# Decoder layer on one core: the order and the filling of TensorE's prologue

## The reference, cut to what matters

```python
def reference(x, ctx_2048, ...):
    x = _layernorm(x + attn(x, qkv_w, qkv_b, ..., proj_w, proj_b, norm_w))   # quantised weights: sign(w) * mean|w|
    x = _layernorm(x + xattn(x, ctx_2048, Wq, Wk, Wv, Wsk, Wsv, Wo))
    x = _layernorm(x + ffn(x, base_w, base_b, router_w, router_b, lora_A, lora_B))
    return x

def _bitlinear(x, w, b):
    w_scale = jnp.maximum(jnp.mean(jnp.abs(w)), 1e-05)
    x_scale = jnp.maximum(jnp.max(jnp.abs(x), axis=-1, keepdims=True), 1e-05)
    x_q = jnp.round(x / x_scale * 127.0)
    return jnp.einsum('...i,oi->...o', x_q, jnp.sign(w)) * (x_scale * w_scale / 127.0) + b
```

## Time and profile before

| what | value |
|---|---|
| median of 3 runs | 913.03 us (912.97 to 913.53) |
| the profiled execution | 913.3 us |
| its span | 911.2 us |
| PE busy | 802.1 us (88%) |
| DVE busy | 509.5 us (56%) |
| ACT busy | 326.4 us (36%) |
| DMA, whole span | 27.10 MB, mean 30 GB/s |

### The profile page before, as it was taken

How to read it: one execution, slowest core, us unless ns; L and a number is a source line. 1 busy time by engine, 2 the same in 40 slices (tenths; PEclk the granted TensorE clock), 3 DMA queues, 4 the chain that set the end, 5 groups by cost and what they waited for, 6 DMA issues and landing times.

```text
span 911.2 us, 22548 instructions
## 1 busy us (share of the span) xinstructions
PE 802.1 (88%) x10161; PEld 524.5 (58%) x10209; DVE 509.5 (56%) x1060; ACT 326.4 (36%) x424; POOL 85.5 (9%) x103
## 2 busy tenths in 40 slices
PE   3788878888998989988998989988998979999996
PEld 2466763477445864577445864577445864486443
DVE  4756584448745593748745593648745582435143
ACT  5534224333245224433245224433245124310422
POOL 1111011000300021000300021000300010010001
PEclk9989999999999999999999999999999999997998
DMA  9921000100002000010002000010001000000000
GB/s 345 246 55 47 2 2 1 47 2 2 2 1 70 3 2 1 26 47 2 1 1 71 3 2 1 27 46 1 1 1 48 2 1 1 24 1 1 1 24 23
DMA packets 19022, 27.10 MB, mean 30 GB/s; under 512 B 5608, under 2 KB 7784, under 8 KB 18928
## 3 DMA queue, kind: packets, MB, share of 16 engines
q1 hardware_dynamic: 18784, 25.64, 9.1%
q10 hardware_dynamic: 144, 0.03, 0.0%
HBM read 21.47 MB, written 4.19 MB: 28 GB/s over the span
## 4 chain that ended last, share of the span: by engine, by line
PE 63%; DVE 19%; ACT 12%; issue 4%; POOL 1%; DMA 1%; ACTq 0%; POOLq 0%; SPq 0%; DVEq 0%
ACT p_b L761 7%; PE ps L1148 7%; PE ps L1184 6%; PE ps L1065 6%; PE ps L1225 6%; DVE max_b L1487 6%; PE ps L1113 4%; PE ps L1048 3%; PE ps L1085 3%; PE ps L893 2%; DVE max_a L1385 2%; PE ps L968 2%; PE ps L1173 2%; PE ps L1157 2%; PE ps L978 2%
## 5 line engine op out<-in xcount | busy, mean ns | idle before, releaser
L761 ACT ACTIVATE p_b<-ps 128x2048 f32<-128x2048 f32 x64 | 106.5, 1664 | 115.9 <-PE ps L1157 115.9
L1487 DVE TENSOR_REDUCE max_b<-ps 128x4 f32<-128x768 f32 (+2 forms) x160 | 106.6, 711 | 31.1 <-PE ps L1127 19.3
L1363 DVE SCALAR_TENSOR_TENSOR nat<-ps,st_a,qkv_bias 128x512 f32<-128x512 f32 x48 | 35.7, 744 | 98.0 <-PE ps L893 96.8
L1113 PE MATMUL ps<-qk_b 32*128 32x192 f32 (+2 forms) x1024 | 65.5, 341 | 22.9 <-DVE max_b L1487 16.8
L1148 PE MATMUL ps<-qk_b 32*128 32x512 f32 (+1 forms) x512 | 66.2, 586 | 9.7 <-ACT p_b L761 5.2
L1113 PEld LDWEIGHTS ps<-qk_b 32*128 32x128 f32 x1024 | 46.2, 188 | 39.9 <-DVE max_b L1487 27.3
L1225 PE MATMUL ps<-base_t,x_t 128*128 128x512 f32 x128 | 63.8, 624 | 0.0
L1173 PE MATMUL ps<-p_b,v_b 128*32 128x256 f32 (+1 forms) x1024 | 61.7, 358 | 2.4 <-ACT p_b L761 2.0
L1048 PE MATMUL ps<-c_t,wq 128*128 128x256 f32 x256 | 60.6, 385 | 2.4 <-DVE out_a L1408 2.3
L1065 PE MATMUL ps<-x_t,wq 128*128 128x256 f32 x256 | 61.3, 385 | 0.0
L1184 PE MATMUL ps<-wo,o_fb 128*128 128x512 f32 x128 | 59.0, 599 | 0.8 <-DVE o_fb L1529 0.8
(11 more groups left out here) (207 smaller groups left out, 1432.7 us busy)
## 6 DMA issues: line engine op xcount, KB each, us to landing
x_in<-x SPq DMA_DIRECT2D x8, 512.0 KB, 5.4
p_b<-ctx SPq DMA_DIRECT2D x8, 512.0 KB, 4.6
y<-x SPq DMA_DIRECT2D x7, 512.0 KB, 3.3
p_b<-L_attn_qkv_w SPq DMA_DIRECT2D x2, 1024.0 KB, 6.5
p_b<-L_xattn_Wq SPq DMA_DIRECT2D x1, 2048.0 KB, 14.9
x<-L_attn_qkv_w SPq DMA_DIRECT2D x2, 512.0 KB, 9.5
x<-L_ffn_base_w SPq DMA_DIRECT2D x2, 512.0 KB, 10.2
wo<-L_xattn_Wo SPq DMA_DIRECT2D x8, 128.0 KB, 9.1
```

Of the source, the lines that this page charges most:

```text
L761: act.activation(p_b[:, j % 2, :, 0:cols], ps[:, 4:8, 0:cols], ACT.Exp, scale=DB ** -0.5).then_inc(pb_here.sem, 1)
L1113: pe.matmul(bank(4 + r)[:, (i % 2) * N:(i % 2) * N + 2 * n * S], q_b[strip[r], i, :, :].rearrange("p h q -> p (h q)"), k_b[strip[r], half, ...
L1363: dve.scalar_tensor_tensor(nat[:, t, w, :], bank(nat_bank(b, w)), st_a[:, 2, t:t + 1], qkv_bias[:, w * C:(w + 1) * C], ALU.mult, ALU.add). ...
L1487: ins = dve.tensor_reduce(max_b[:, half, 0, i:i + k, 2 * n:2 * n + 2], ps[:, 4 + 2 * n:6 + 2 * n, :].rearrange("p r (i n) -> p i r n", i=2 ...
```

## The change

Two things change, all in the prologue and all on PE. `a1(0)` moves ahead of `early` in PE's list. And a helper `warm(n)` is added, n matmuls of the identity with itself repeated four times (512 columns, bfloat16) into bank 7. It runs 22 of them ahead of the wait for the signs of piece 0, 3 ahead of piece 1, 11 ahead of a1(0)'s wait for the rounded x, and 3 in `early` ahead of the wait for the third piece.

```diff
+            def warm(n):
+                for _ in range(n):
+                    pe.matmul(bank(7).rearrange("p (a n) -> p a n", a=4), eyeb, eyeb.unsqueeze(1).to_broadcast([P, 4, P]), start=True, stop=True)
+
             for n in range(2):
+                warm((22, 3)[n])
                 pe.wait_ge(signed.sem, n + 1)
                 sign_turn(n)
...
             def early(b):
+                warm(3)
                 pe.wait_ge(signed.sem, 4)
                 sign_turn(2)
                 pe.wait_ge(cf_in.sem, 16)
...
             def a1(b):
+                if isinstance(b, int) and b == 0:
+                    warm(11)
                 x_round(pe, b)
                 za_here.before(pe, b)
...
-            first = [(-1, early), (0, a1), (0, of(a1_qkv, 0, [0])), (0, of(a1_qkv, 0, [1])), (0, of(a1_qkv, 0, [2])), (0, of(a1_qkv, 1, [0])),
+            first = [(0, a1), (-1, early), (0, of(a1_qkv, 0, [0])), (0, of(a1_qkv, 0, [1])), (0, of(a1_qkv, 0, [2])), (0, of(a1_qkv, 1, [0])),
```

## The result

| runs of one set | kernel before, median | changed kernel, median | ratio, 95% interval |
|---|---|---|---|
| first set, 20 and 20 runs | 915.22 us (911.13 to 915.94) | 911.16 us (907.95 to 914.61) | 0.9970 (0.9958 to 0.9982) |
| second set ("again"), 29 and 12 runs | 913.17 us | 912.75 us | 0.9989 (0.9974 to 1.0005) |
| third set ("again2"), 32 and 12 runs | 913.70 us | 910.75 us | 0.9971 (0.9958 to 0.9983) |

The account below looks back on a forecast made before the run. The prediction took the chain up to 31 us, with PE not its only engine, as the bound. Terms 2.7 + 0.5 + 0.6 = 3.8, less 0.4, gave 3.4 us: 913.0 to 909.6 us, range 907.2 to 912.3 us.

Parts of the forecast that it names:

- What bounds the kernel: Up to 31 us: PE is not alone on the chain; x's transposes wait 3.6 us for work they don't need.
- The fill ahead of piece 0: Prologue: 22 fills from 3.3 to 10.2 us raise the clock, costing 0.5 us on the chain (bounds 0 and 3.0).
- The move of x: Prologue: x transposed under ACT's signs, so the first real matmul begins at 18.6 us instead of 21.30, 2.7 us earlier.
- DVE becomes the bound: After the first nat: DVE sets the pace, the sixth nat ending at 27.5 instead of 31.28 us, 3.8 us earlier.
- What is late next: Behind the sixth nat, to L837: the ctx load and the clock's fall do not move with the chain; 0.4 us lost.
- the cap of 4.9 us: At ctx's landing, 51.4 us: the load costs nothing up to a total gain of 4.9 us, and caps it there.
- the 0.4 us set against it: Score matmuls at 44.8 us (old time): 1.1 us lost if the clock falls before them, otherwise nothing; taken as 0.4.
- The sum: Whole kernel: 2.7 + 0.5 + 0.6 = 3.8, less 0.4, a gain of 3.4 us, from 913.0 to 909.6 us.
- the term for the late part: The rest of the program, eight batches: no transfer is waited for, so it should follow unchanged.
- A worse late part: Rival, low clock at 817 to 831 us: the stretch grows or another appears, some 3 us back, 912.6 us; chance 0.07.
- The slower rival: Prologue: identity products don't raise the clock, fills delay everything, 5.3 us slower, 918.3 us; chance 0.05.
- Nothing arrives: Rival: a later wait that doesn't move takes up the prologue's shift, leaving 913 us; chance 0.05.

Follow-up runs that it names:

- again: The changed kernel run once more, unaltered, against the kernel before: 912.75 us, ratio 0.9989.
- again2: The changed kernel run unaltered another time, on one chip with three rivals, against the kernel before: 910.75 us, ratio 0.9971.
- fill12: The changed kernel with 12 fills instead of 22 ahead of piece 0: 910.42 us, ratio 0.9963 to the kernel before.
- fill12_tail: The changed kernel with 12 first fills, plus five keep_on matmuls ahead of the last batch's first score group: 909.89 us, ratio 0.9954.
- fill_turns: The changed kernel with each fill matmul of 512 columns replaced by 4 transposes of 128 columns: 912.81 us, ratio 0.9990.

## Why the prediction was right or wrong

**What bounds the kernel.** Right. The transposes of x waited for work that they don't need. One reading was wrong, without a consequence for the sum: what lands at 8.83 us is the second weight piece. The first was there at 6.1 us, which this row of ACT in the kernel before shows:

```profile
6.12 1.91 ACT L599 ACTIVATE x_t<-p_b 128x2048 bf16<-128x2048 f32 x1 [3.67 <-DMA p_b<-L_attn_qkv_w]
```

The order alone takes the start from 145.0 to 141.7 us.

**The fill ahead of piece 0.** Begin 3.3 (3.55 us), end 10.2 (10.3 us), piece 0's copy 11.3 (11.23 us): right for this profile. But the identity's load was taken as a fixed 2.6 us; it was 2.8 and 4.0 us in two profiles of the same kernel, and the fills began between 3.33 and 4.92 us in six. The lower level lasted for a varying part of the 22: they took 6.34 to 7.57 us. The cost on the chain was 0.5 us forecast; by fill12 it is 0 to 1.5 us, within the bounds that the prediction gave.

**The move of x.** The 11 fills did not start behind piece 1's transposes but at 13.25 us, behind ACT's first copy, which PE's program waits for there; x was transposed from 15.62 us, still under ACT's signs. Forecast 18.6 us for the first real matmul, 17.92 us measured. ACT's copy of x began at 16.66 us, since it overlaps the end of the signs, and the 0.51 us between the copy and the first matmul, which I carried over from the earlier trace rows, were 0.24 us; what made up the 0.51 us was not looked into. The first nat was at 19.06 us (forecast 19.7).

**DVE becomes the bound.** Nearly right. The sixth nat's end was forecast at 27.5 us, and measured at 26.2. DVE had one wait of 0.26 us, ahead of the sixth nat; from the first nat to the sixth's end it took 7.15 us with that wait, and not 7.75 us, because nat and L1373 overlap by some 0.1 us where I had added gaps. Both engines end together here.

**What is late next.** The ctx load was waited for, 0.62 us, under the cap of 4.9 us, as forecast. The fall of the clock came with the idle stretch, as forecast; the 0.4 us set against it can't be seen apart. From the sixth nat (5.1 us) to the start (4.7 us) 0.4 us were lost in this profile.

**The sum.** Forecast 3.4 us; at the start, the mean of six profiles of the changed kernel (141.1 us) is 3.9 us under the mean of four of before (145.0 us), from 2.4 to 5.4 us by pairs. The mechanism and its size at the start were right, and two errors offset each other in it: the sixth nat came 4.7 us earlier on average (30.6 and 25.9 us) and not 3.8, and 0.7 us of that were lost before the start and not 0.4.

**The step that failed** is the term for the late part and the base under it. The sum put the late part at nothing ("should follow unchanged") and took 913.03 us as the base, both on one ground: "The three runs agree within 0.6 us, so it is steady from run to run". They agreed by chance. Single runs of the kernel before go from 910.9 to 916.1 us with the median of the first set at 915.22 us, and its late part takes 69.8 or 71.3 us. So 913.03 us was no fair base. A worse late part, which I priced at 3 us and gave 0.07, is common: 1 profile in 6 of the changed kernel, 1 in 4 of before and 10 in 10 of the other kernels, at 1.0 to 3.3 us each. That the measured 911.16 us is only 1.6 us from the forecast is in part luck: the gain was taken from a base that was 2.2 us too low.

How much of the gain at the start the late part took back is worked out and not shown. The means are 911.7 us (44 runs) and 914.0 us (116 runs). Less 2.1 us outside the span, 696.3 us, and the starts of 141.1 and 145.0 us, that leaves late parts of 72.2 and 70.6 us. By this working the start gained 3.9 us and the late part gave back 1.6 us, which makes the 2.3 us between the means. It rests on starts read in six and four profiles, and these are no fair sample: the six profiled executions of the changed kernel took 909.9 us on average, 1.8 us under its mean of all runs, and the four of before 913.7 us, 0.3 us under. Later starts in the runs without a profile would do as well. Why a shift at the start would lengthen the late part on average, and whether it does beyond chance, stays open.

**The slower rival** (products of the identity don't raise the clock) is out: the 22 fills took 6.34 to 7.57 us in six profiles of the changed kernel, where at the lower level 9.4 us would have passed. "Nothing arrives" is out as well.

## What to carry to other kernels

Take a step that waits in an engine's queue behind work it does not need, and move it; that was worth 3.3 of 3.9 us at the start here, without one extra instruction. Fill matmuls that keep the clock up must end before the data that the engine waits for, and when they end hangs on the load that they start from and on when the clock rises. And before a base time is trusted to a few tenths of a per cent, look at whether the time has more than one length; find two marks in the trace by which the span splits, and compare kernels mark by mark.

## What the runs showed of the hardware that I had not expected

- Transposes raised TensorE's clock as matmuls of the same columns did: 88 of 128 columns in 7.5 us, at the lower level 9.4 us would have passed.
- The place of the clock's rise moved from run to run of the same kernel: the first 11 real matmuls took 2.62 and 3.78 us in two profiles of the order alone, and 4.25 to 4.87 us in four of the kernel before.
- The granted clock fell with PE busy for 5.72 of 6 us (fill12_tail, 816.8 us), most of its matmuls having 32 or 3 rows, and it stayed at 0.50 for 7 to 14 us with PE busy nearly all of the time (15.00 of 15 us in the changed kernel).
- The same 32 KB load, first in its queue, took 2.3 us (fill_turns), 2.8 (changed), 4.0 (again) and 4.2 us (again2).
- The late part's low clock came in stretches of about 7, 10 and 14 us; no profile of the 20 is without one, and where there are two the late part is 1.0 to 3.3 us longer.
